# Row maxima of attention scores: one VectorE reduction over two neighbouring PSUM banks, and one signal a step

## What is computed

```python
energy = einsum("nhqd,nhkd->nhqk", q, k)
attn   = softmax(energy / sqrt(16), axis=-1)
out    = einsum("nhqk,nhkd->nhqd", attn, v)
x      = layernorm(x + out)
```

## Time and profile before

| | us |
|---|---|
| median of 3 runs | 7127.48 |
| lowest, highest | 7126.87, 7132.86 |
| the profiled execution | 7131.26 |
| its span, first to last instruction | 7129.5 |
| phase A, B, C, D, about | 1331, 1897, 1680, 1818 |

### The profile page before, as it was taken

One profiled execution on the slowest core, in us unless ns is written; L12 is line 12 of the kernel. 1 busy time (PEld: TensorE's weight loads), 2 busy tenths in 40 slices (PEclk: granted clock), 3 DMA queues, 4 the chain that ended last, 5 costly groups with the idle time before them and its releaser, 6 DMA issues. The chain is left out here.

```text
span 7129.5 us, 143478 instructions
## 1 busy us (share of the span) xinstructions
PE 5831.5 (82%) x54804; PEld 3904.2 (55%) x54914; DVE 5463.8 (77%) x12626; ACT 3784.8 (53%) x6869; POOL 2616.1 (37%) x2600
## 2 busy tenths in 40 slices
PE   6899898688888787876999999999118888888887
PEld 4666566454545455544666666666105666666655
DVE  6777777578888888887777777777657888888886
ACT  4666666444555555553565565556105555555554
POOL 0111111122222222232434434544315666656664
PEclk9999999888888888887999999999658999999998
DMA  1111111100000000000000000100100000000000
GB/s 54 37 44 40 42 38 37 43 15 23 23 20 23 20 23 19 24 21 26 29 25 27 30 27 24 32 27 22 35 17 24 18 27 21 22 27 18 27 27 12
DMA packets 140386, 194.36 MB, mean 27 GB/s; under 512 B 25808, under 2 KB 63696, under 8 KB 139344
## 3 DMA queue, kind: packets, MB, share of 16 engines
q1 hardware_dynamic: 139728, 185.26, 8.2%
HBM read 113.03 MB, written 72.18 MB: 26 GB/s over the span
## 5 line engine op out<-in xcount | busy, mean ns | idle before, releaser
L1079 DVE TENSOR_REDUCE Dmp<-pj 128x2 f32<-128x512 f32 x1024 | 647.1, 683 | 145.5 <-PE pj L794 143.4
L1079 DVE TENSOR_REDUCE Amp<-pj 128x2 f32<-128x512 f32 x1024 | 644.7, 683 | 136.0 <-PE pj L794 135.6
L1079 DVE TENSOR_REDUCE Cmp<-pj 128x2 f32<-128x512 f32 x1024 | 643.2, 683 | 90.0 <-PE pj L794 89.5
L932 ACT ACTIVATE Dpr<-st 128x512 f32<-128x512 f32 x1024 | 528.8, 603 | 314.4 <-PE st L729 313.5
L932 ACT ACTIVATE Apr<-st 128x512 f32<-128x512 f32 x1024 | 528.7, 602 | 288.2 <-PE st L729 286.5
L932 ACT ACTIVATE Cpr<-st 128x512 f32<-128x512 f32 x1024 | 529.5, 606 | 250.5 <-PE st L729 249.1
L1014 POOL TENSOR_SCALAR Bve<-Bmv 128x2 f32<-128x2 f32 x128 | 29.6, 231 | 1346.0 <-DVE Bmv L1145 1346.0
L1014 POOL TENSOR_SCALAR Ave<-Amv 128x2 f32<-128x2 f32 x64 | 14.7, 229 | 1141.2 <-DVE Amv L1145 1141.2
L990 POOL TENSOR_TENSOR Dnrm<-Dnrm,power 128x32 f32<-128x32 f32 x64 | 348.6, 5447 | 161.7 <-DVE Dnrm L1057 161.7
L729 PE MATMUL st<-Dq,Dk 32*128 32x256 f32 x4096 | 361.7, 433 | 51.0 <-DVE Dq L1086 40.4
L932 ACT ACTIVATE Bpr<-st 77x512 f32<-77x512 f32 x512 | 262.0, 593 | 191.5 <-PE st L729 190.8
(11 more groups left out here) (310 smaller groups left out, 15817.8 us busy)
## 6 DMA issues: line engine op xcount, KB each, us to landing
Ax0T<-in_xT SPq DMA_DIRECT2D x64, 256.0 KB, 2.6
Ax<-in_x SPq DMA_DIRECT2D x64, 256.0 KB, 2.9
x_A_scratch<-Ax SPq DMA_DIRECT2D x64, 256.0 KB, 2.0
Bx<-x_A_scratch SPq DMA_DIRECT2D x64, 256.0 KB, 2.9
x_B_scratch<-Bx SPq DMA_DIRECT2D x64, 256.0 KB, 2.0
Cx<-x_B_scratch SPq DMA_DIRECT2D x64, 256.0 KB, 2.8
x_C_scratch<-Cx SPq DMA_DIRECT2D x64, 256.0 KB, 2.0
Dx<-x_C_scratch SPq DMA_DIRECT2D x64, 256.0 KB
```

The lines of the kernel that those rows point to most:

```text
L932: ck.tell(act.activation(dst, st[bank][0:n, :], ACT.Exp, scale=HD ** -0.5), "probs_ready", step)
L1079: ins = dve.tensor_reduce(dst, src, AX.X, ALU.max, negate=True)
```

## The change

The four banks become one tensor `pj_all` of 128x4x512, and `pj[i]` are views of it. On VectorE a `max` step waits for both of its banks. If they are neighbours, one `tensor_reduce` reads both and writes the maxima of both (128x2x2 out of two banks; 128x4x2 in A2). If they are banks 3 and 0, there are still two reductions. The lower-numbered bank now holds head 0. In all cases there is a single `max_done` for the step, on its last reduction, and it frees both banks. The work of TensorE is the same.

```diff
-        "max": ["max_done"] * 2,
+        "max": ["max_done"],
...
     if kind == "max":
-        return "max_done", use[:-1], use[-1]
+        return "max_done", use[:-1], -1
...
-        pj = [stack.enter_context(nc.psum_tensor(f"pj{i}", [P, HALF], F32)) for i in range(BANKS)]
+        pj_all = stack.enter_context(nc.psum_tensor("pj", [P, BANKS, HALF], F32))
+        pj = [pj_all[:, i] for i in range(BANKS)]
...
+                def pair(self, step):
+
+                    return sorted([step + (0,), step + (1,)], key=self.number)
...
-                        for i in range(2):
-                            ck.wait_bank_free(step + (i,))
+                        uses = ck.pair(step)
+                        for use in uses:
+                            ck.wait_bank_free(use)
...
-                        for i, heads in enumerate(max_heads(att, step[3])):
-                            m, (c, p0, e) = len(heads), place(heads[0])
-                            ck.wait_bank_full(step + (i,))
...
-                            ins = dve.tensor_reduce(dst, src, AX.X, ALU.max, negate=True)
-                            ck.tell(ins, "max_done", step)
+                        uses = ck.pair(step)
+                        low, high = (ck.number(use) for use in uses)
+                        for use in uses:
+                            ck.wait_bank_full(use)
...
+                        src = [pj_all[:, low:high + 1]] if high == low + 1 else [pj_all[:, b:b + 1] for b in (low, high)]
...
+                        for i, banks in enumerate(src):
+                            n = 2 // len(src)
+                            ins = dve.tensor_reduce(
+                                dst[:, n * i:n * i + n], banks.rearrange("p b (h t n) -> p b h t n", h=m, t=QT)[:, :, :, :, 0:KEYS[att]],
+                                AX.X, ALU.max, negate=True)
+                        ck.tell(ins, "max_done", step)
```

More of the change, by code:

```diff
@@ L583, in bank, with number @@
                     return pj[counts.bank[self.latest[step], use][0]]
+                def number(self, use):
+                    return counts.bank[self.latest[use[:-1] if use[0] in ("gu", "max") else use], use][0]
+                def pair(self, step):
+                    return sorted([step + (0,), step + (1,)], key=self.number)
                 def wait_bank_full(self, use):
@@ L793, in do @@
                                     first = (QT * hh + t) * S // len(heads[i])
-                                    ins = pe.matmul(ck.bank(step + (i,))[:, first:first + n],
+                                    ins = pe.matmul(ck.bank(uses[i])[:, first:first + n],
                                                     qb[e][s][p0:p0 + 32, c, t * P:(t + 1) * P],
@@ L797, in do @@
                                     if (hh, t) == (len(heads[i]) - 1, QT - 1):
-                                        ck.filled(ins, step + (i,))
+                                        ck.filled(ins, uses[i])
                     elif kind == "shift":
@@ L1071, in do @@
                     elif kind == "max":
-                        for i, heads in enumerate(max_heads(att, step[3])):
-                            m, (c, p0, e) = len(heads), place(heads[0])
-                            ck.wait_bank_full(step + (i,))
-                            first = c * P + p0 + 16 * (1 - e)
-                            dst = mp[s][:].rearrange("p t c n -> p t (c n)")[:, :, first:first + 16 * m - 15:16]
-                            src = ck.bank(step + (i,))[:].rearrange("p (h t n) -> p t h n", h=m, t=QT)[:, :, :, 0:KEYS[att]]
-                            ins = dve.tensor_reduce(dst, src, AX.X, ALU.max, negate=True)
-                            ck.tell(ins, "max_done", step)
+                        heads = max_heads(att, step[3])
+                        m, (c, p0, e) = len(heads[0]), place(heads[0][0])
+                        uses = ck.pair(step)
+                        low, high = (ck.number(use) for use in uses)
+                        for use in uses:
+                            ck.wait_bank_full(use)
+                        first = c * P + p0 + 16 * (1 - e)
+                        src = [pj_all[:, low:high + 1]] if high == low + 1 else [pj_all[:, b:b + 1] for b in (low, high)]
+                        step_ = 32 // m
+                        dst = mp[s][:].rearrange("p t c n -> p (c n) t")[:, first:first + step_ * (2 * m - 1) + 1:step_, :].rearrange(
+                            "p (b h) t -> p b h t", b=2)
+                        for i, banks in enumerate(src):
[4 more added lines that the diff above has]
+                        ck.tell(ins, "max_done", step)
                     elif kind == "shift":
```

## The result

The changed kernel takes **7307.83 us** (median of 4 runs, 7306.0 to 7312.16) against 7128.71 for the kernel before (4 runs, 7126.87 to 7132.86): ratio 1.0251, 95% interval 1.0234 to 1.0269. It is 179 us slower. The forecast was 7230, with a range of 7170 to 7325: the direction and the mechanism were as forecast, the size was 1.8 times the +100 that I took, near the upper end of the range.

The account below looks back on a forecast made before the run. No engine is saturated; a chain changing engines, mostly through TensorE, was taken to bound each phase. 7131.3 - 16 (shorter reductions) + 116 (late releases, 95 on the chain and 21 beside) = 7231, stated as 7230 us; range 7170 to 7325.

Parts of the forecast that it names:

- the +100: Whole kernel: net cost chosen between +79 and +201 us, a sixth of the way up.
- The -16 us on the chain: VectorE's maxima: five whole pairs a round on the chain, 64 rounds, 73% fused, 0.07 us saved each: -16 us.
- The late release: First bank of a fused step comes free 0.53 us later (0.32 in B), delaying TensorE: +95 us on the chain.
- What lies beside the chain: TensorE's tight waits off the chain: partly swallowed by idle time behind them, 21 us.
- That is the upper bound.: All phases: 430 tight TensorE starts after a first reduction, their delays all in series: 217 us.
- +79 is what no overlap takes away, only a changed TensorE clock could.: Old chain with its new lengths, each engine's order fixed: 95 - 16 = +79 us must be felt.
- The clock's return: TensorE's clock in A, B and D: returning half of what they lose, 30 us, gives 7180 at the lower end.
- slower still, by the clock: Rival: more TensorE gaps give each body one more stretch at 1.2 GHz, 102 us on top: 7333; chance 0.10.
- my sign of being wrong, over 50: TensorE's busy time up by over 50 us would mean clock stretches, not releases, made the difference.
- Faster: Rival: early releases don't matter, only shorter VectorE work is left: 7115 us, or 7039 with all on the path; chance 0.05.
- no change: Rival: shifted or removed 1.2 GHz stretches give back what the releases cost in each round: about 7130; chance 0.06.
- It doesn't do what it says: Rival: the fused instruction needs 1.28 us, the 16 us are gone and releases 0.07 later: 7259; chance 0.06.

Follow-up runs that it names:

- the kernel with one signal at the 12 steps: Kernel before, but at 12 max steps a round whose first release lay on the traced chain only the second reduction signals; nothing fused: 7204.21 us, ratio 1.0104.
- the one with everything else: Changed kernel, but 12 max steps a round whose first release lay on the traced chain keep two reductions and two signals: 7243.18 us, ratio 1.0154.
- the one with 30 steps early: Changed kernel, but the 30 max steps a round on banks 3 and 0, which it doesn't fuse, keep two signals: 7285.10 us against 7130.94, ratio 1.0211.

## Why the prediction was right, and where it was not

- **Fused duration.** Right. Taken at 1.21 us between 1.21 and 1.28, and 0.79 in B: measured 1.221 and 0.793. The row of another operand in another memory was good to 1%.
- **VectorE's saving.** Forecast 92 us of its busy time, measured 66. By the rows of the reductions it is 0.044 us a fused step instead of 0.07. 0.011 of the difference is the longer instruction. The rest lies in that a reduction's end overlaps the start of the next one: in an unbroken run those of 0.683 start 0.598 us apart, two of them 1.20, and the fused ones 1.14. The estimate of 0.157 us, from the (N+151)/0.96 ns that the Trainium skill gives for one fp32 `tensor_tensor` (VectorE: DVE Perf Modes, "The TRN2 errata"), is not borne out for these consecutive reductions.
- **The -16 us on the chain.** Not seen in the changed kernel, which is 16 us slower than the one that only signals late. Where the fused steps delay nobody, 46 of 82 brought 13 and 3 us in two comparisons, and those of A and D alone nothing clear of noise.
- **The late release.** Right, and this is the mechanism. Forecast as the cause, 0.53 us at a fused step. Shown by the kernel that has only the late signal: 165 of 179 us. Right too: TensorE's waits for the maxima grew most in C.
- **What lies beside the chain: the term that was mis-sized.** I took 21 us for it, a sixth of the way from the chain to all tight waits, on the word that other waits have idle time behind them. By the kernel with one signal at the 12 steps, and the one with everything else, it is as large as the chain's own term: 88 us (165 - 77) or 116. The chain view shows one of several that end nearly together. The measured +179 lies four fifths of the way from +79 to +201. By phase, with the prediction's own sums (us, without the -16):

  | | A | B | C | D |
  |---|---|---|---|---|
  | on the chain | 25 | 18 | 35 | 17 |
  | all tight waits in series | 52 | 32 | 87 | 46 |
  | measured | 44 | 0 | 88 | 51 |

  C, with the clock near full, pays for all its tight waits, A for most, B for none. D pays more than all of them, but most of it as busy time at the lower clock. That the total came out inside the range owes something to luck, for B's nothing offsets part of what C and D cost above the forecast.
- **"That is the upper bound."** It left out users that come a little later. Paired again from the trace before, some 140 first banks more have their next user 0.18 to 0.6 us after the release. They are delayed in part, by an estimate of 30 us in sum.
- **"+79 is what no overlap takes away, only a changed TensorE clock could."** It was taken away in part. In the kernel with the 12 late signals A's 29 came out as 18 while its clock rose from 0.95 to 0.97, which fits the exception in the sentence. In B the +18 came out as 0 in the changed kernel too, at an unchanged clock of 0.87, so there the clock isn't shown to have paid. The step that failed is taking a chain that I had followed through one body of B as one whose delays must be felt; what absorbs them stays open. The clock's return stood only in the lower end of the range, half of what A, B and D lose, and not in the forecast itself.
- **The rival "slower still, by the clock".** It came in part: D's clock fell to 0.93 and its busy time on TensorE rose by 43 us, C's clock to 0.98. TensorE's busy time rose by 60 us on the page (5831.5 to 5891.2; the windows above show +64), so my sign of being wrong, over 50, was met. I said that it would mean that clock stretches, not releases, made the difference. That reading was wrong: the kernel with only the late signals lost 165 us with 23 us more of it (5831.5 to 5854.7), 45 more in D and less in A and C. In D the late signals alone bring the lower clock, 0.93.
- **Faster, and no change:** ruled out by the interval of 1.0234 to 1.0269. "It doesn't do what it says" too: 1312 fused instructions are in the trace.
- **Body lengths.** "C some 2 us longer" was 6 (104.5 to 110.5); A went from 81.9 to about 85; D did not keep 109.2 but went to 112.6, and stayed there as exactly as before.

What stays open: why C's clock is 0.98 and 0.97 in the changed kernel and the one with 30 steps early, but 0.99 in the one that only signals late and in the one that keeps 12 steps early; what absorbs the delay in B; and what decides at which length B and D settle. No run here holds the clock fixed.

## To carry to other kernels

Merging two reads of a double buffer into one also merges their releases: before fusing, look who takes the first buffer and when. Here an instruction fewer was worth 0.04 to 0.05 us of VectorE's time, and giving a bank back 0.53 us later cost up to the whole of that at each user that stood waiting. If the chain of waits runs through such places, count the tight ones beside it as well: in this kernel, with its fixed order, they were about as expensive. Fuse only where the next user is late, and expect little even then.

## What the hardware showed that I had not expected

- Phase B keeps its length. With delays between 0 and about 1.2 us in each body (an estimate, three late releases) it stays at 1825 to 1828 us in ten kernels, in seven of them at 1827.6 to 1828.1. Where a delay of 0.61 us was added alone, the granted clock over the phase rose from 0.87 to 0.89, that is, TensorE stood less time at 1.2 GHz, which could pay for it; in the changed kernel it stayed at 0.87, so this can't be the whole reason.
- Where the bodies of D and B have a steady length, it is one of two: 109.2 and 112.6 in D, 116.05 and 119.5 in B. It isn't a rule for every kernel: D varies between 110.6 and 113.3 us from body to body with the 12 late signals, and B between 117 and 119.6 with 2.4 us added.
- A reduction over two neighbouring banks runs at the rate of one over SBUF: 1.221 and 1.211 us for 1024 numbers in the changed kernel.
